# Silu of z behind softplus, the sums of the mixer's sum dropped, and ScalarE's other work moved between groups

## The reference

```python
x = x + _layernorm(_L0_attn_ref(_layernorm(x, axis=-1), ...), axis=-1)
x = x + _layernorm(_L0_ffn_ref(_layernorm(x, axis=-1), ...), axis=-1)
```

```python
dt = jax.nn.softplus(dt @ dt_proj_w + dt_proj_b)
dA = jnp.exp(dt[..., None] * A[None, None])
dBx = dt[..., None] * Bm[:, :, None, :] * xc[..., None]
h = dA_t * h + dBx_t
y_t = jnp.einsum('bds,bs->bd', h, C_t)
y = (y + xc * D[None, None, :]) * jax.nn.silu(z)
y = y @ out_proj_w + residual
```

## Time and profile before

| | |
|---|---|
| median of 3 runs | 2746.5 us |
| lowest, highest | 2743.5, 2748.03 us |
| the profiled execution | 2747.34 us |
| its span, first to last instruction | 2745.5 us |
| mean granted clock of PE | 0.953 |
| ACT busy | 1632.7 us, 59% of the span |
| POOL busy | 1509.0 us, 55% |
| DMA | 352.38 MB, mean 128 GB/s |

### The profile page before, as it was taken

How to read it: one execution, slowest core, us unless ns; L and a number is a source line. 1 busy time by engine, 2 the same in 40 slices (tenths; PEclk the granted TensorE clock), 3 DMA queues, 4 the chain that set the end, 5 groups by cost and what they waited for, 6 DMA issues and landing times.

```text
span 2745.5 us, 27113 instructions
## 1 busy us (share of the span) xinstructions
PE 2421.4 (88%) x8416; PEld 1183.9 (43%) x8416; DVE 2439.3 (89%) x3235; ACT 1632.7 (59%) x3312; POOL 1509.0 (55%) x546
## 2 busy tenths in 40 slices
PE   4556799998989999898999999899999989888988
PEld 1112254453545445454544445454444545443554
DVE  1699999999999999999999999999999999999642
ACT  3565656666665667666566667656576655654331
POOL 0255465655556565655656565565656556565511
PEclk9677899999999999999999999999999999999999
DMA  1623253534435353534435353443535344352321
GB/s 36 230 83 125 94 180 92 182 115 144 127 126 164 112 162 118 175 99 140 151 115 162 122 176 88 152 140 115 182 97 177 117 137 129 112 170 87 85 58 59
DMA packets 174892, 352.38 MB, mean 128 GB/s; under 512 B 16252, under 2 KB 81565, under 8 KB 166301
## 3 DMA queue, kind: packets, MB, share of 16 engines
q1 hardware_dynamic: 164668, 334.93, 36.6%
q0 software_dynamic: 10080, 15.73, 3.5%
HBM read 291.35 MB, written 51.38 MB: 125 GB/s over the span
## 4 chain that ended last, share of the span: by engine, by line
DVE 58%; issue 17%; ACT 15%; PE 10%; DMA 0%; POOL 0%; DVEq 0%; SPq 0%; ACTq 0%; POOLq 0%
DVE hs L909 26%; DVE hs L895 12%; DVE th L1019 5%; DVE th L1024 4%; PE Gp L432 2%; PE Up L440 2%; PE MY L450 2%; ACT DX L538 2%; DVE XC L868 2%; ACT dA L520 2%; ACT L520 1%; PE FP L359 1%; PE FP L369 1%; ACT XC L591 1%; ACT SZ L596 1%
## 5 line engine op out<-in xcount | busy, mean ns | idle before, releaser
L795 POOL TENSOR_TENSOR hs<-hs,Cb 128x2048 f32<-128x2048 f32 x256 | 1170.6, 4573 | 200.1 <-DVE hs L895 200.1
L520 ACT ACTIVATE dA<-dtr,A 128x512 f32<-128x512 f32 x1024 | 701.8, 690 | 822.6 <-DVE hs L909 821.2
L775 POOL TENSOR_TENSOR th<-th,cmb 128x512 f32<-128x512 f32 x256 | 337.8, 1325 | 819.8 <-DVE hs L895 713.4
L909 DVE TENSOR_TENSOR_SCAN hs<-dA,carry,hs 128x512 f32<-128x512 f32 x512 | 628.5, 1265 | 19.9 <-ACT dA L520 19.5
L909 DVE TENSOR_TENSOR_SCAN hs<-dA,hs 128x512 f32<-128x512 f32 x512 | 596.4, 1204 | 34.5 <-ACT dA L520 34.0
L432 PE MATMUL Gp<-x2T,Wgu 128*128 128x512 f32 x1024 | 531.8, 644 | 105.3 <-DVE th L1019 105.3
L895 DVE TENSOR_TENSOR hs<-dxr,Bb 128x2048 f32<-128x2048 f32 x256 | 603.9, 2359 | 12.5 <-DMA dxr<-dx_d 12.5
L440 PE MATMUL Up<-x2T,Wgu 128*128 128x512 f32 x1024 | 493.4, 605 | 0.0
L450 PE MATMUL MY<-Wdn,th 128*128 128x256 f32 x2048 | 485.8, 381 | 0.8 <-POOL th L775 0.8
L450 PEld LDWEIGHTS MY<-Wdn,th 128*128 128x128 f32 x2048 | 383.9, 190 | 136.1 <-issue 92.9
L432 PEld LDWEIGHTS Gp<-x2T,Wgu 128*128 128x128 f32 x1024 | 181.9, 196 | 439.8 <-issue 248.8
(11 more groups left out here) (133 smaller groups left out, 1824.3 us busy)
## 6 DMA issues: line engine op xcount, KB each, us to landing
dtr<-dt_d SPq DMA_DIRECT2D x64, 1024.0 KB, 5.6
dxr<-dx_d SPq DMA_DIRECT2D x128, 512.0 KB, 7.3
cmb<-cm_d SPq DMA_DIRECT2D x256, 256.0 KB, 3.7
Wdn<-in_w_dn SPq DMA_DIRECT2D x256, 128.0 KB, 3.6
dt_d<-XB SPq DMA_DIRECT2D x16, 1024.0 KB, 4.3
dx_d<-DX SPq DMA_DIRECT2D x16, 1024.0 KB, 5.8
Bb<-bc_d SPq DMA_DIRECT2D x64, 256.0 KB, 3.1
Cb<-bc_d SPq DMA_DIRECT2D x64, 256.0 KB, 4.0
```

What stands on the lines that cost most here:

```text
L520: act.activation(dA[h % 2][:, :], dtr[:, M % 2, beta, :], ACT.Exp, scale=A[:, k:k + 1]).then_inc(s_dA, 1)
L775: pool.tensor_tensor(th[:, q % NTH, :], th[:, q % NTH, :], cmb[:, q % 2, :], ALU.mult).then_inc(m_a, 1)
L795: pool.tensor_tensor(hs[:, G % NH, :, :], hs[:, G % NH, :, :], Cb[:, s, :].unsqueeze(1).broadcast_to([P, NBETA, CH]), ALU.mult).then_inc(s ...
L909: dve.tensor_tensor_scan(hv, dA[h % 2][:, :], hv, first, ALU.mult, ALU.add).then_inc(s_h, 1)
```

## The change

1. In the second layer norm of P the four sums and the scaling are gone. The negative mean of x1 is taken from the one of x, which E had computed two chunks earlier and which is now kept for all chunks in a tile `x_nm` (128 x 16 x 4).
2. ACT's steps move. z0's copy goes from group 6 to the end of group 4; z1's copy from the middle of group 10 to the middle of group 7; z2's and z3's copies from group 11 to the end of group 9, ahead of softplus; Silu of z from the end of group 12 to directly behind softplus; the x2 normalisation (`p_x2`) from the end of group 6 to the middle of group 7; the input's normalisation (`e_norm`) from group 7 to group 8.
3. PE's fills move with them: z0 to the end of group 4, z1 to group 6, z2 to group 9 before `down`, z3 and then the fill for softplus (`db`) behind `down` of group 9. `FILLS` and `f_act` get the new order.

DVE, POOL and SP issue the same instructions in the same places.

```diff
-FILLS = ['b2', 'k2', 'r0', 'r1', 'b3', 'k3', 'z0', 'xp', 'x0', 'x1', 'rt', 'db', 'z1', 'ct', 'z2', 'z3', 'xT0', 'xT1', 'b0', 'b1']
+FILLS = ['b2', 'k2', 'r0', 'r1', 'b3', 'z0', 'k3', 'z1', 'xp', 'x0', 'x1', 'rt', 'z2', 'z3', 'db', 'ct', 'xT0', 'xT1', 'b0', 'b1']
...
-        e_s = sb('e_s', [P, 3, TB])
+        e_s = sb('e_s', [P, 2, TB])
+        x_nm = sb('x_nm', [P, NC, TB])
...
-                if F and g in (0, 4, 6, 11):
-                    f_in(p, {0: 'b2', 4: 'b3', 6: 'z0', 11: 'z3'}[g])
+                if F and g in (0, 4, 6, 9):
+                    f_in(p, {0: 'b2', 4: 'b3', 6: 'z1', 9: 'z2'}[g])
...
-                if F and g == 9:
-                    f_dt(p)
...
-                if F and g in (9, 10):
-                    f_in(p, f'z{g - 8}')
+                if F and g == 4:
+                    f_in(p, 'z0')
+                if F and g == 9:
+                    f_in(p, 'z3')
+                    f_dt(p)
...
-            def p_sums2(p):
...
+            def p_squares2(p):
...
-                sums(x1[:, (p - 1) % 2, :, :], b_s, dx_half).then_inc(p_act.sem, 1)
-
-            def p_squares2(p):
-                squares(x1[:, (p - 1) % 2, :, :], b_s, p_act, p - 1, 'sum2', dx_half).then_inc(p_act.sem, 1)
+                act.wait_ge(e_dve.sem, e_dve.at(p - 1, 'w1'))
+                squares(x1[:, (p - 1) % 2, :, :], b_s, x_nm[:, p - 1, :], dx_half).then_inc(p_act.sem, 1)
...
-                if F and g in (10, 11):
-                    f_z(p, g - 9)
+                if F and g == 7:
+                    f_z(p, 1)
+                if R_ and g == 7:
+                    p_x2(p)
...
                 if R_ and g == 5:
-                    p_sums2(p)
                     p_squares2(p)
...
-                if F and g in (6, 11):
-                    f_z(p, {6: 0, 11: 3}[g])
+                if F and g == 4:
+                    f_z(p, 0)
                 if F and g == 6:
                     f_silu(p)
-                if R_ and g == 6:
-                    p_x2(p)
                 if F and g == 7:
                     f_xd(p)
-                if in_e(p) and g == 7:
-                    e_norm(p + 2)
                 if R_ and g == 8:
                     p_x2T(p, 1)
+                if in_e(p) and g == 8:
+                    e_norm(p + 2)
                 if F and g == 9:
+                    f_z(p, 2)
+                    f_z(p, 3)
                     f_softplus(p)
+                    f_silu_z(p)
...
-                if F and g == 12:
-                    f_silu_z(p)
...
-                shift(p_dve, p_nb, b_s, p_w)
+                shift(p_dve, p_nb, x_nm[:, c, :], p_w)
```

More of the change, by code:

```diff
@@ L149, in sandwich_kernel @@
         p_s = sb('p_s', [P, 3, TB])
-        b_s = sb('b_s', [P, 3, TB])
+        b_s = sb('b_s', [P, 2, TB])
         p_w = sb('p_w', [P, 3, TB])
@@ L169, in sandwich_kernel @@
         e_act = Steps(sem('e_act'), ['sum', 'nm', 'sq', 'xr'])
-        f_act = Steps(sem('f_act'), ['xT0', 'xT1', 'raw0', 'tap0', 'raw1', 'tap1', 'raw2', 'tap2', 'raw3', 'tap3', 'z0', 'silu_x', 'xd', 'dt', 'z1', 'z2', 'z3', 'silu_z'])
+        f_act = Steps(sem('f_act'), ['xT0', 'xT1', 'raw0', 'tap0', 'raw1', 'tap1', 'raw2', 'tap2', 'raw3', 'z0', 'tap3', 'silu_x', 'z1', 'xd', 'z2', 'z3', 'dt', 'silu_z'])
         f_dve = Steps(sem('f_dve'), [f'c{k}{m}' for m in DVE_CONV for k in range(HIST)] + ['hist', 'dx'])
@@ L175, in sandwich_kernel @@
         p_dve = Steps(sem('p_dve'), ['w1', 'nb', 'Bw1'] + rsqrt_names('q') + ['Bnb'] + route)
-        p_act = Steps(sem('p_act'), ['xn0', 'xn1', 'rev0', 'rev1', 'nm', 'sq', 'ro', 'sum2', 'nm2', 'sq2', 'x2', 'x2T0', 'x2T1', 'sig', 'cmT'])
+        p_act = Steps(sem('p_act'), ['xn0', 'xn1', 'rev0', 'rev1', 'nm', 'sq', 'ro', 'sq2', 'x2', 'x2T0', 'x2T1', 'sig', 'cmT'])
         m_g, m_u, m_d, m_th, m_v, m_w, m_a = (sem(k) for k in ('m_g', 'm_u', 'm_d', 'm_th', 'm_v', 'm_w', 'm_a'))
@@ L526, in tanh, with sums, squares, means_squares @@
                 act.activation(th[:, q % NTH, :], Gp[:, :], ACT.Tanh, scale=0.5).then_inc(m_th, 1)
-            def sums(x, s, to=None):
+            def sums(x, s):
                 for b in range(TB):
-                    ins = act.activation(to[b] if to else x[:, b, :], x[:, b, :], ACT.Copy, accum_out=s[:, 0, b:b + 1])
+                    ins = act.activation(x[:, b, :], x[:, b, :], ACT.Copy, accum_out=s[:, 0, b:b + 1])
                 return ins
-            def squares(x, s, steps, c, n, waste):
+            def squares(x, s, nm, waste):
+                for b in range(TB):
+                    ins = act.activation(waste[b], x[:, b, :], ACT.Square, bias=nm[:, b:b + 1], accum_out=s[:, 1, b:b + 1])
+                return ins
+            def means_squares(x, s, nm, steps, c, n, waste):
                 act.wait_ge(steps.sem, steps.at(c, n))
-                act.activation(s[:, 2, :], s[:, 0, :], ACT.Copy, scale=-1.0 / DM).then_inc(steps.sem, 1)
+                act.activation(nm, s[:, 0, :], ACT.Copy, scale=-1.0 / DM).then_inc(steps.sem, 1)
                 act.wait_ge(steps.sem, steps.at(c, n) + 1)
-                for b in range(TB):
-                    ins = act.activation(waste[b], x[:, b, :], ACT.Square, bias=s[:, 2, b:b + 1], accum_out=s[:, 1, b:b + 1])
-                return ins
+                return squares(x, s, nm, waste)
             dx_half = [flat[:, (TB + b) * DM:(TB + b + 1) * DM] for b in range(TB)]
@@ L550, in e_squares @@
                     act.wait_ge(st_dx, 16 * min(c - 1, NC))
-                squares(xin, e_s, e_act, c, 'sum', dx_half).then_inc(e_act.sem, 1)
+                means_squares(xin, e_s, x_nm[:, c, :], e_act, c, 'sum', dx_half).then_inc(e_act.sem, 1)
             def e_norm(c):
@@ L635, in p_squares @@
                 act.wait_ge(e_act.sem, e_act.at(min(p + 2, NC - 1), 'sq'))
-                squares(rn, p_s, p_act, p - 1, 'rev1', dx_half).then_inc(p_act.sem, 1)
-            def p_sums2(p):
+                means_squares(rn, p_s, p_s[:, 2, :], p_act, p - 1, 'rev1', dx_half).then_inc(p_act.sem, 1)
+            def p_squares2(p):
                 if p < NC:
@@ L691, in z_squares @@
                 act.wait_ge(f_dve.sem, f_dve.at(min(c + 3, NC - 1), 'dx'))
-                squares(my, z_s, z_act, c, 'my', xb_half).then_inc(z_act.sem, 1)
+                means_squares(my, z_s, z_s[:, 2, :], z_act, c, 'my', xb_half).then_inc(z_act.sem, 1)
             def z_norm(c):
@@ L838, in variance, with shift @@
                 dve.tensor_scalar(w[:, 0, 0:TB], s[:, 1, :], 1.0 / DM, LN_EPS, ALU.mult, ALU.add).then_inc(steps.sem, 1)
-            def shift(steps, nb, s, w):
-                dve.tensor_tensor(nb[:, :], s[:, 2, :], w[:, 1, 0:TB], ALU.mult).then_inc(steps.sem, 1)
+            def shift(steps, nb, nm, w):
+                dve.tensor_tensor(nb[:, :], nm, w[:, 1, 0:TB], ALU.mult).then_inc(steps.sem, 1)
             def e_var(c):
@@ L852, in e_scale @@
                 dve.tensor_scalar(ln1[:, c, 0, :], rs, 1.0, None, ALU.mult).then_inc(e_dve.sem, 1)
-                dve.tensor_tensor(ln1[:, c, 1, :], e_s[:, 2, :], rs, ALU.mult).then_inc(e_dve.sem, 1)
-                dve.tensor_tensor(e_nb[:, :], e_s[:, 2, :], rr, ALU.mult).then_inc(e_dve.sem, 1)
+                dve.tensor_tensor(ln1[:, c, 1, :], x_nm[:, c, :], rs, ALU.mult).then_inc(e_dve.sem, 1)
+                dve.tensor_tensor(e_nb[:, :], x_nm[:, c, :], rr, ALU.mult).then_inc(e_dve.sem, 1)
             def ep_newton(k, c0, c1):
@@ L922, in p_scale @@
             def p_scale(p):
-                shift(p_dve, p_nb, p_s, ep_w)
+                shift(p_dve, p_nb, p_s[:, 2, :], ep_w)
             def p_scale2(p):
@@ L1030, in z_scale @@
                 newton(z_dve, c, 'r', z_w)
-                shift(z_dve, z_nb, z_s, z_w)
+                shift(z_dve, z_nb, z_s[:, 2, :], z_w)
             def last_x1():
```

## The result

The changed kernel takes **2779.86 us** (median of 4 runs, 2775.68 to 2781.79), the kernel before 2746.34 in the same session. The ratio is 1.0121, its 95% interval 1.0104 to 1.0139: slower, by 33 us, as forecast (2783, range 2754 to 2804). The profiled execution took 2775.68 us with a span of 2773.9, 28.4 more than before's 2745.5.

What follows compares the result with a forecast made beforehand. DVE was taken as the bound, so only its waits counted. Thirteen steady chunks +25, period 0 +7.5 and period 1 +4 gave +36.5 on 2747.34, so 2783.8; less 0.8 to the median, 2783 us, range 2754 to 2804.

Steps and rivals of the forecast that it cites:

- group 7 wait: Scans' wait for a decay behind Silu of x; exp table back 2.6 us earlier, so its 0.85 us goes.
- expert gate of group 8: New wait of about 0.5 us for tanh, as z1's copy and the x2 normalisation now stand in group 7.
- third scan of group 10: New wait of 3.9 us for its decay, behind group 9's serial fills, copies, softplus and Silu; bounds 2.5 and 5.8.
- period 0: No routing covers group 9 and PE runs at 1.2 GHz: wait of 1.83 grows to about 11; +7.5 us net.
- period 1: Routing but a slow clock and no experts in group 9: taken as +4 us.
- after the last scan: Period 15 and the tail lose the sums (1.9 us) before a busy PE: 0, at best -1.
- rival B: Faster: ACT's work sets the pace; third scan of group 10 waits below 1.95 us; 2738 us; chance 0.12.
- Rival C: Slower still: PE idles some 7 us, loses clock, gate and up in group 11 double; 2800 us; chance 0.12.
- Rival D: No change: new waits just pay for those removed, group 10 waiting about 1.4 to 1.9; 2747 us; chance 0.08.
- The forecast on 1.28: Group 9's table loads counted at 1.28 us each without a drain; with the skill's drain, near 2837 us.
- so its wait of 1.60 is gone: Group 13: no Silu or table load left there, so 1.60 us was booked as saved per steady chunk.
- Head ... the dx transfer starts about 8 us later: Before the first scan: z1 to z3 now precede dt; set against the 9.08 us wait for ACT: 0, -1 to +5.

Runs made afterwards that it cites:

- Experiment 1: The changed kernel with Silu of z alone put back to the end of group 12: 2738.71 us.
- experiment 3: The kernel before with only the four sums and their scaling dropped: 2746.48 us.
- experiment 7: experiment 6 with POOL's output DMA of group 13 issued behind `read_out`: 2727.95 us.
- experiment 2: The changed kernel with POOL's output DMA of group 13 issued behind `read_out` instead of ahead: 2775.41 us.
- experiment 6: The changed kernel with z1 copied at the end of group 6, z2 in group 7, z3 before softplus, z3 and db filled ahead of down: 2740.69 us.
- experiment 8: experiment 7 with POOL's DMA of x1 in group 5 issued behind `weigh` instead of ahead of it: 2729.03 us.
- 9: experiment 7 with POOL's DMA of x1 in group 5 issued behind `read_out`: 2731.19 us.

## Why the prediction was right, and where it was not

The sum beside what the two traces show, in us. A period runs from its first scan to that of the next; "steady" is the mean of periods 2 to 14.

| term | forecast | measured |
|---|---|---|
| group 7 wait | -0.85 | -0.85, -0.99 in even periods |
| group 13 wait | -1.60 | -1.60, -1.72 |
| expert gate of group 8 | +0.5 | +0.34, +0.40 |
| third scan of group 10 | +3.9 | +3.41, +3.88 |
| group 6 wait, not counted | 0 | -0.40 in odd periods |
| product of group 13, not seen | 0 | +1.29 |
| a steady chunk | +1.95 | +2.30 (158.23 to 160.53) |
| thirteen of them | +25 | +29.9 |
| period 0 | +7.5 | +5.9 |
| period 1 | +4 | +2.5 |
| head, to the first scan | 0 | -8.1 |
| after the last scan | 0 | -1.9 |
| all | +36.5 | +28.4, as the spans |

**The mechanism was right.** Group 9's slack did not hold the second excursion behind two copies and their fills. Experiment 1 shows that by itself: Silu of z in group 12 costs 1.60 there, and behind softplus it raises the wait of group 10 from 0.42 to 3.67 on average. The total of the scans' wait is 64.7, not the 85 named: the head's 9.08 is gone from it, which the 85 still held, period 0 added 8.0 and not 9, and the steady wait was 0.23 smaller (13 times that is 3). These make 13 of the 20; the rest is in small waits that I did not follow up.

**The number was in part luck.** It came out 3 us from the forecast, although the collision, about 17 us over the thirteen chunks, was not in the sum, and the head and the stretch behind the last scan, 10 us together, were booked at 0.

**Drops of ACT work are worth nothing** (experiment 3), and rival B's condition, a wait under 1.95, was met in no steady period. *Rival C* was right in what happens and wrong in its price: PE does lose its clock behind the gap. Kernel after:

```profile
950.00:970.00 20.00, 13.16 (x45) 5.65 (x45) 16.59 (x15) 12.77 (x16) 10.47 (x4) 0.83 0.35 126
970.00:990.00 20.00, 15.18 (x50) 7.11 (x49) 18.94 (x28) 12.89 (x32) 11.63 (x6) 0.83 0.37 119
```

Granted 0.83, part of each stretch at 1.2 GHz; yet no scan of group 11 waits for ACT, and the wait of group 12 is what it was.

**Rival D and the table load.** Rival D needed a wait of 1.4 to 1.9 in group 10, and it was 3.41 or more. A load takes 1283 ns, and Silu starts 0.02 after it, at 954.45 behind 953.15 + 1.28. The load before softplus at 949.05 ran in the wait for db's fill, which ended at 950.21. The forecast on 1.28 held, and no drain was seen.

**Step that failed: "so its wait of 1.60 is gone"**, taken as 1.60 won. The wait is gone, but what lay under it, `read_out` still running, then lengthened the product by 1.29: the net gain of group 13 was 0.4 on average. The prediction asked what covers each edit it booked at nothing; it did not ask what the removed wait itself covered. The evidence was in the trace of before: POOL's late `read_out` ended 0.46 ahead of the product, and in group 5, where no wait stands, the product takes 3.27 on average. The Trainium skill has the rule (SBUF — State Buffer, section SBUF: two separate sides): a DVE instruction with two SBUF inputs and a GpSimd one that reads SBUF hold one shared port pair exclusively, and the later one waits. The rows agree to 0.12 us: an overlap of 1.24 cost 1.12, of 0.99 cost 0.87, of 0.34 cost 0.21. In all eleven traces every product that overlaps a `read_out` by more than 0.12 us, 562 of them, is longer by that overlap less 0.12 to 0.14, and without such an overlap none is longer than 2.33. Scans beside `read_out` take their usual 1.2; they read dA from PSUM.

**Step that failed: "Head ... the dx transfer starts about 8 us later"**, and so 0. The product that makes dx (DVE L887) started at 73.38, against 72.30: 1.1 later. ACT and PE in the head, kernel after the earlier trace rows:

```profile
65.98 0.60 ACT L590 ACTIVATE SZ<-FP 128x512 f32<-128x512 f32 x1
68.65 0.60 ACT L590 ACTIVATE SZ<-FP 128x512 f32<-128x512 f32 x1 [2.07 <-PE FP L360]
...
85.08 1.30 ACT L522 ACTIVATE dA<-dtr,A 128x512 f32<-128x512 f32 x2
```

```profile
55.89 1.98 PE L360 MATMUL FP<-xT,Win 128*128 128x512 f32 x4 [0.78 <-ACT XC L585]
...
66.63 1.98 PE L360 MATMUL FP<-xT,Win 128*128 128x512 f32 x4 [0.69 <-ACT SZ L590]
```

I took before's waits of 3.87 along with the fills, and they did not come along. z1's fill now lies beside the load and Silu of x, and z2's and z3's take 1.98, at the full clock, instead of 3.78. The projection to dt, B and C ahead of them also took 3.62 instead of 6.37, at a granted clock of 1.00 instead of 0.50, which paid for one of the two; before it PE had stood idle 4.00 us, now 1.78. Before, PE had stood idle 4.87 us for softplus just ahead of them, and the granted clock was 0.50; its timeline, and the two stretches that follow:

```profile
72.32 3.78 PE L359 MATMUL FP<-xT,Win 128*128 128x512 f32 x4 [4.87 <-ACT XB L610]
```

```profile
70.00:76.00 6.00, 3.68 (x4) 1.17 (x4) 2.29 (x1) 2.27 (x4) 0.00 (x0) 0.50 0.47 174
76.00:82.00 6.00, 4.63 (x6) 1.67 (x6) 0.00 (x0) 1.19 (x2) 0.00 (x0) 0.50 1.03 345
```

So ACT had its decays ready at 85.1 instead of 97.7, and the first scan, at 90.36, now waits for the input product alone. The clock of the moved work was a term, and I sized it by the old place. That is read from the two traces; no run changed the clock alone.

**Period 0 and 1** were each forecast 1.5 too high. The scan of period 0 waits 9.79, forecast 11. About 2 us of that is Silu's place: in experiment 1 the same scan still waits 7.64.

**Why the same edit paid 12.7 us in experiment 7 and 4.5 in experiment 2.** It is no backlog of PE from group 10: in all traces PE is caught up at the gate of group 13, 0.14 behind the first scan, after 3.3 to 4.8 us of idle time in the steady periods. From there to the gate of group 5 PE has no gap in either, and needs 76.63 us after, 76.60 in experiment 2, 76.68 in experiment 6 and 75.95 in experiment 7 (means of periods 2 to 13). So freeing DVE's product left PE's stretch as it was in experiment 2 and shortened it by 0.73 in experiment 7, beside the 0.79 by which the chunk fell. In the 20 us behind that gate the granted clock was 0.87 in experiment 2 and 0.90 in experiment 7.

**What stays open.** No run varied PE's clock alone, so that the clock makes the difference of 0.65 is not shown. The terms of a steady chunk in the table add up to 2.6 (means over periods 2 to 14), where the chunks grew by 2.30. Most of the rest is that DVE's scans took 0.17 less in a chunk, and the product of group 5 0.06; no run says why.

## What to carry to other kernels

Before a wait is booked as won, look at what other engines do during it: it may keep two instructions apart that exclude each other. Ask of each stretch of the loop which engine has no gap there; a saving on another engine in that stretch may only make its next wait longer, as in experiment 8. A step moved next to a like one, to save a switch, is paid at the wait that ends the new, longer chain, so count the slack there first, and take the duration of a moved matmul at the clock of its new place.

## What the runs showed that was not expected

- DVE's f32 product of two SBUF operands is longer by the time that it lies beside POOL's `read_out`, less 0.12 us (experiments 2, 7, 8 and 9, and every trace). Scans are not.
- The issue of a DMA takes POOL 0.9 to 1.3 us. `weigh` behind it starts while the issue still runs and is recorded at 1.60 to 1.79 instead of 1.28, though `read_out` follows its start by 1.23, as elsewhere; `read_out` itself is slower, 4.83 to 5.03 instead of 4.53.
- 38 us of ACT's work could go without an effect that could be measured (experiment 3), while the place of one 1.9 us activation was worth 41 us (experiment 1).
